# Nineteen matmuls on constants around the first transposes of an attention and expert-layer kernel

## What is computed

```python
def fake_quant(x, scale, zp):
    q = jnp.clip(jnp.round(x / scale + zp), 0, 255)
    return (q - zp) * scale

x = x + jnp.matmul(fake_quant(_layernorm(x), x1_scale, x1_zp),
                   fake_quant(ctx_4096, x2_scale, x2_zp))

h = _layernorm(x)
weights, selected = jax.lax.top_k(jnp.einsum('bsd,ed->bse', h, gate_w), 2)
weights = jax.nn.softmax(weights, axis=2)
w_full = jnp.sum(jax.nn.one_hot(selected, 8) * weights[..., None], axis=2)
result = jnp.einsum('bsd,od->bso', h, base_w) + base_b
low = jnp.einsum('bsd,erd->ebsr', h, lora_A)
x = x + result + 2.0 * jnp.einsum('ebsr,eor,bse->bso', low, lora_B, w_full)
```

## Time and profile before

| | us |
|---|---|
| median of 3 runs | 180.59 |
| lowest and highest of them | 180.41, 181.01 |
| the profiled execution's own time | 179.92 |
| its span, first to last instruction | 178.0 |

### The profile page before, as it was taken

The page is one execution under the profiler, slowest core; times in us unless marked ns, Lnnn a source line. Parts: engine busy times, 40 slices in busy tenths (PEclk is TensorE's granted clock), DMA queues, the critical chain, the costliest instruction groups (busy, mean ns, idle before and its releaser), DMA issues.

```text
span 178.0 us, 2466 instructions
## 1 busy us (share of the span) xinstructions
PE 167.0 (94%) x862; PEld 124.1 (70%) x862; DVE 123.3 (69%) x314; ACT 77.3 (43%) x132; POOL 16.2 (9%) x33
## 2 busy tenths in 40 slices
PE   5818999899999999999999999999999999999992
PEld 1314454479888888886788668876888688888881
DVE  0789948999999999799968834866856268411233
ACT  2269977995236096557432631339131101140100
POOL 3021204110010000000050101021010000100000
PEclk9995899999999999999999999999999999999999
DMA  5999999999993019803099426059118020420033
GB/s 108 395 420 411 367 412 348 272 256 217 414 345 59 0 64 295 351 2 120 32 220 205 89 47 118 0 96 198 63 17 221 4 93 25 76 41 4 0 118 118
DMA packets 9515, 29.55 MB, mean 166 GB/s; under 512 B 1184, under 2 KB 1184, under 8 KB 9504
## 3 DMA queue, kind: packets, MB, share of 16 engines
q1 hardware_dynamic: 7344, 22.06, 33.3%
q0 software_dynamic: 2016, 7.34, 21.9%
q10 hardware_dynamic: 144, 0.00, 0.0%
HBM read 22.05 MB, written 4.19 MB: 147 GB/s over the span
## 4 chain that ended last, share of the span: by engine, by line
PE 86%; DVE 9%; DMA 2%; issue 1%; ACT 1%; DVEq 0%; ACTq 0%
PE ps_even L929 25%; PE ps_odd L929 25%; PE ps_att L875 12%; PE ps_g L911 6%; PE ps_t L859 4%; PE ps_even L883 3%; PE ps_g L914 2%; DMA q_in<-in_scales 2%; DVE x_sb L617 2%; PE ps_t L850 2%; DVE stats L559 1%; PE ps_odd L972 1%; PE ps_even L972 1%; PE ps_even L971 1%; PE ps_odd L971 1%; PE ps_odd L970 1%
## 5 line engine op out<-in xcount | busy, mean ns | idle before, releaser
L929 PE MATMUL ps_even<-w_hi,yt 128*128 128x512 f32 x128 | 37.7, 397 | 0.0
L929 PE MATMUL ps_odd<-w_hi,yt 128*128 128x512 f32 x128 | 36.7, 403 | 0.0
L875 PE MATMUL ps_att<-c,c1t 128*128 128x512 f16 x96 | 25.7, 391 | 1.8 <-DVE c L606 1.8
L929 PEld LDWEIGHTS ps_odd<-w_hi,yt 128*128 128x128 f32 x128 | 23.5, 188 | 5.0
L929 PEld LDWEIGHTS ps_even<-w_hi,yt 128*128 128x128 f32 x128 | 23.5, 188 | 4.9
L929 PE MATMUL ps_even<-w_lo,yt 128*128 128x512 f32 x64 | 20.1, 391 | 0.0
L929 PE MATMUL ps_odd<-w_lo,yt 128*128 128x512 f32 x64 | 19.3, 393 | 0.0
L875 PEld LDWEIGHTS ps_att<-c,c1t 128*128 128x128 f16 x96 | 8.9, 100 | 11.6 <-issue 2.7
L351 ACT ACTIVATE ln_v<-mv,eps 128x1 f32<-128x1 f32 x16 | 4.7, 292 | 28.5 <-DVE mv L564 28.5
L911 PE MATMUL ps_g<-ag,yt 128*128 128x272 f32 x64 | 16.8, 336 | 0.0
L642 DVE TENSOR_TENSOR yt<-ps_t,yt 128x512 fp32r<-128x512 f32 x15 | 10.3, 685 | 9.2 <-ACT yt L420 9.0
(11 more groups left out here) (99 smaller groups left out, 259.7 us busy)
## 6 DMA issues: line engine op xcount, KB each, us to landing
ring<-in_ctx SPq DMA_DIRECT2D x12, 512.0 KB, 8.4
w_raw<-in_w_t SPq DMA_DIRECT2D x8, 512.0 KB, 9.5
x_sb<-in_base_b POOLq DMA_DIRECT2D x8, 512.0 KB, 5.9
out_x<-x_sb SPq DMA_DIRECT2D x16, 256.0 KB, 2.0
x_sb<-in_x SPq DMA_DIRECT2D x7, 512.0 KB, 6.2
x_sb<-zfix POOLq DMA_DIRECT2D x6, 512.0 KB, 6.3
x_sb<-in_ctx SPq DMA_DIRECT2D x4, 512.0 KB, 7.8
ag_raw<-in_ag_t SPq DMA_DIRECT2D x1, 544.0 KB, 6.6
```

The lines of the kernel that those rows point to most:

```text
L875: ins = pe.matmul(att_bank(t)[h][:, :], c1t[:, t % 4, k, :], c2[:, k, h * HALF:(h + 1) * HALF], start=(k == 0), stop=(k == CT - 1))
L929: pe.matmul(ffn_bank[t % 2][h][:, :], rows_of(part, t, k), w[:, k, h * HALF:(h + 1) * HALF], start=start, stop=False)
```

## The change

A helper `keep_warm(n)` issues `n` matmuls of the same form as `warm_up`: 512 columns, the constant `ones` on both sides, into `ps_g`. Fourteen stand between `warm_up()` and `transpose_c1(0)`, five between `transpose_c1(0)` and `attention(0, 0)`. They wait for nothing, signal nothing and their results are not read.

```diff
+            def keep_warm(n):
+                for _i in range(n):
+                    pe.matmul(ps_g[:, :], ones[:, :], ones[:, :].unsqueeze(1).broadcast_to([P, HALF // P, P]),
+                              start=True, stop=True)
...
             pe.wait_ge(consts, 4)
             warm_up()
+            keep_warm(14)
             transpose_c1(0)
+            keep_warm(5)
             attention(0, 0)
             attention(0, 1)
             column_sums_first(0)
```

## The result

The changed kernel takes 182.94 us (median of 7 executions), the kernel before 180.41 beside it. The ratio is 1.0104, 95% interval 1.0070 to 1.0138: **slower, by about 1.9 us**. An execution more than 1.5% above the fastest of its own kernel (here three of the change's seven and one of the seven before) is left out of this and all later ratios, but not out of the medians and ranges, which is why the medians lie 2.5 apart. The profiled execution of the change took 180.82 us (179.92 before) and is the fastest of its seven, so it shows the loss at its smallest.

A forecast was written before the change was run, and what follows sets the result against it. PE was taken to bound the kernel, slowed by its clock. Clock -1.7 and waits for a later DVE +3.7 gave +2.0 on 179.92, so 181.9; with part of the median's extra 0.67, 182.0 us, range 179.5 to 183.0.

The forecast's parts named there:

- The added matmuls: Fourteen behind warm-up end at 11.4, five behind the transposes at 13.3; both lie in PE's idle time: cost 0.
- the rival of the late constants: The fourteen end behind 11.6 and delay the transposes; gain and penalty shrink, 180 to 181.5 us; chance 0.03.
- the waits for DVE that the prediction had counted: PE in tile 0 waits for DVE's integers of tile 1 (15.95) and context block 7 (22.77), limiting gain to 1.7 of 2.7.
- The clock and PE's gain: With the clock staying at 2.4 GHz, PE finishes tile 0's attention at 24.1 instead of 25.7: gain 1.7 us.
- The sharing: POOL's `zfix` DMAs, issued 1.5 us earlier, take turns from the weight loads: 2.1 us later per microsecond.
- The term of 3.0 us: Later landing of the last weight block because sharing of the DMA engines starts earlier; bounds 0 and 3.2.
- upper bound of 3.2: Largest delay of the last weight block, if sharing starts the full 1.5 us earlier: landing at 44.6 instead of 41.5.
- the 44.5 of the forecast: Landing time of the last weight block, 3.0 us behind the 41.5 of the kernel before.
- Who waits for the block: ACT, then DVE, wait for the last weight block and hold PE up at tile 1's expert matmuls: 2.0 us later.
- the prediction's -1.0: At tile 1's expert matmuls, if the last block still lands at 41.5, PE keeps 1.0 us of gain.
- The wait at `base_high(0, 7)`: PE, due there at 44.0, can start at 45.6; this wait of 1.6 us adds nothing to the end.
- the forecast +2.0: Net change at the end of the profiled execution: -1.7 us from the clock, +3.7 from waits for a later DVE.

The follow-up runs named there:

- only5: Changed kernel without the fourteen added matmuls, so only the five between the first transposes and the first attention step: 183.00 us, ratio 1.0096 to the kernel before.
- only14: Changed kernel without the five added matmuls, so only the fourteen behind warm-up: 183.68 us, ratio 1.0194 to the kernel before.
- after_swap: Changed kernel with ACT's `split_y_hi(1, 0)` moved ahead of the high part of weight block 7: 182.30 us, ratio 1.0073 to the kernel before.
- after_b: Changed kernel with the experts' second factor loaded early, right behind weight block 7, and POOL's DMAs not held: 183.49 us, ratio 1.0117 to the kernel before.
- after_hold2: Changed kernel with POOL's two `zfix` DMAs waiting until weight block 2 has landed: 179.88 us, ratio 0.9969 to the kernel before.
- after_hold3: Changed kernel with POOL's two `zfix` DMAs waiting until weight block 3 has landed: 180.03 us, ratio 0.9935 to the kernel before.
- after_hold3_b: Changed kernel with POOL's `zfix` DMAs waiting for weight block 3 and the experts' second factor loaded early: 178.90 us, ratio 0.9899 to the kernel before.
- the hold to block 7: Changed kernel with POOL's two `zfix` DMAs waiting until the last weight block has landed: 187.81 us, ratio 1.043 to the kernel before.
- before_hold3: Kernel before, without added matmuls, with POOL's two `zfix` DMAs waiting until weight block 3 has landed: 179.24 us, ratio 0.9953 to the kernel before.

## Why the prediction was right, point by point

**The time.** 182.0 with the range 179.5 to 183.0 was forecast, 182.94 was measured, just inside the upper end. The forecast step was +1.4 us on the median of 180.59; measured are +1.9 by the ratio and +2.5 by the medians of the same day.

**The added matmuls cost nothing themselves.** Right for the end, though not at the spot. The slow part of warm-up (matmuls of 634 ns in the trace, 379 ns after it) lasted to 7.9 here instead of 5.8, so that the fourteen ended late and the transposes began at 12.28 instead of 11.61. This is the rival of the late constants, and it cost 0.2 us at the attention (14.21), since ACT took up the copy at 13.06 instead of 12.86. By the end of tile 0 the 0.2 is gone, in the waits for DVE that the prediction had counted.

**The clock and PE's gain.** Right: no slow stretch, tile 0 done at 24.1 (23.25 + 0.86), forecast 24.1; 1.6 us gained, forecast 1.7. `zfix` at 23.64, forecast 23.6. POOL's issue at 25.37, forecast 25.3. That both gaps had to be filled was implied, and was not so in the profiled executions of `only5` and `only14`.

**The sharing.** Right in what it comes to: the rate falls 1.5 us earlier, and the block is late. Wrong in how it starts: what begins 2.4 us behind POOL's issue is not the taking of turns, which begins 5.2 us behind it, but a slowing of the loads alone. The term of 3.0 us was 1.4 in the profiled execution of the change, and in the four others with the same time of issue 3.0 to 4.3, three of them above the upper bound of 3.2. (41.5 and 3.2 are 44.7 and not 44.6.) "Landing" is when ACT takes the block up, less 0.02, or issue plus landing time where ACT did not wait:

| kernel | POOL issues `zfix` | block 7 lands | fifth L911/L916 matmul pair of tile 1 starts, less 52.12 |
|---|---|---|---|
| change | 25.37 | 42.8 | +0.38 |
| only14 | 25.45 | 44.4 | +1.97 |
| after_swap | 25.30 | 45.2 | not behind the block |
| only5 | 25.41 | 45.4 | +2.93 |
| after_b | 25.44 | 45.8 | +3.33 |
| before | 26.82 | 41.5 | 0 |
| after_hold2 | 27.67 | 40.9 | -1.55 |
| after_hold3 | 29.70 | 37.1 | PE limits |
| after_hold3_b | 31.33 | 36.4 | PE limits |

At equal time of issue the landing scatters by 3 us, so one profile was not enough to size this term; the 44.5 of the forecast was inside what the five kernels show (mean 44.7). The rule of the Trainium skill that the prediction weighed (DMA: Bandwidth & Descriptors, Queues, rings and completion order), by which the engines go round the queues packet by packet, agrees with the trace of the change from 31 on (98 packets beside 106 from 31 to 34). It gives neither the scatter of the landings nor the 211 packets of the loads from 28 to 31 with 4 of POOL's beside them; what slows the loads there is open. That it takes POOL's early issue is shown, since with the hold on block 3 they nearly keep their rate to 33.

**Who waits for the block.** Right, and exact: the prediction's -1.0 plus the delay of the block against 41.5 gives +0.3, +1.9, +2.9, +3.3 and -1.6 for the rows of the table whose last column has a number other than 0; measured +0.38, +1.97, +2.93, +3.33 and -1.55. The wait at `base_high(0, 7)` was absent in the change's profile (its block came at 42.8, before the need at 44.0) and was there, 1.2 to 2.3 us, in the four kernels whose block came later.

**What failed.** The sum for the profiled execution: +0.4 at the expert matmuls and +0.4 at 100, against the forecast +2.0, from the sharing term above and from the `zfix` DMA of tile 4, whose room of 0.2 I had not looked for. Two stores of 256 KB and a bias DMA ran beside that DMA in both kernels; why it took 1.3 us longer is open. By the median over executions the first term is nearer to what was forecast. I had also not seen that the clock can fall once more behind the waits for the block, as in the profile of `after_b`. Of the seven executions of the change the three up to 182.74 have a mean clock of 0.999 or 1.000 and the four from 182.94 on 0.988 to 0.991, so a second fall is likely part of why the median lies above 182; none of those four was profiled.

## What to carry to other kernels

When an engine is made earlier, list what its results release, the DMAs above all, and ask what is still in flight at the new time: here a gain of 1.6 us on the bounding engine started transfers 1.5 us earlier, and they delayed the loads that the same engine needed next by 1.4 to 4.3. Where two streams share the DMA engines and one of them has slack, make that one wait for the other's landing, and check what stands in the issuing queue behind it: with the hold to block 3 and an earlier load of one operand the changed kernel was 1.0% faster than before, with the hold to block 7 it was 4% slower. Judge a kernel in which several results come only 0.1 to 0.2 us before they are needed by many executions, since one profile may show any of its ways to wait.

## What was not expected of the hardware

- In the profiled execution of `only5` the clock stays full through 2.8 us of idle PE and eight small transposes when five matmuls of 512 columns follow. Without the five it fell at 13.8 behind 2.7 us of idle and the same transposes in `before_hold3`, and at 12.6 behind 3.25 us in the kernel before. With only the fourteen ahead it stays as well, in the profiled execution of `only14`, through 1.9 us of idle.
- Without added matmuls the slow stretch has two lengths from one execution to the next, with a mean granted clock of 0.981 or 0.990: 6.8 us in the profile of the kernel before, 3.4 in that of `before_hold3`. The warm-up's own slow part ended at 5.8 in one profile and at 7.9 in another of the same first twenty matmuls; the granted clock reads 1.00 in both, all through it.
- The loads slow down 2.4 us behind POOL's issue, from 117 packets in the microsecond from 25 to 58 in that from 29, while no packet of POOL's queue moves.
- The same accumulating DMA of 512 KB, with the same two stores and a bias DMA about it, took 4.9 us in one profiled execution and 6.2 in the other; the last weight block landed between 42.8 and 45.8 for issues of POOL within 0.15 us.
